# Two middle token chunks sorted by expert instead of by group, and late chunks taken between sorted pairs

## The chip, the cores and the metric

The kernel runs on one core of one Trainium2 chip. The metric is the device time of one execution in microseconds (us). Times of single instructions come from one profiled execution.

## What is computed

A vision tower of two layers on 64 images of 64 tokens (4096 tokens of width 256). Patch embedding, attention, a mixture of experts (8 experts in the program, one of them shared, top 2 of 7), a second attention, and a second mixture of experts, in which this change lies for the most part:

```python
# second layer: 16 experts in 4 groups; the best 2 groups, then the best 4 experts of those
scores = sigmoid(xf @ router_weight.T); s_choice = scores + router_bias
gidx   = top_k(sum of the top 2 of each group, 2)
topk   = top_k(s_choice masked to the two groups, 4)
w      = scores[topk] / (sum + 1e-20) * 2.5
out    = sum over e of combine[:, e] * (silu(x @ w_gate[e].T) * (x @ w_up[e].T)) @ w_down[e].T
h      = h + out
```

Products are made of three float32r products (high*high, low*high, high*low), so each tile is split into a high and a low part before it is used.

## The kernel before

Tokens lie in 32 blocks of 128. A mixture phase takes its blocks in chunks (`CHUNKS0` for the first layer, `CHUNKS` for the second). Work runs in pairs of two blocks. An "own" pair takes two blocks in token order: it is turned (transposed), gets its router logits, and in the first layer also the shared expert. When all own pairs of a chunk are through, DVE works out the routing of the chunk (`routing`, or `choose_experts` to `weigh_experts` in the first layer), and GpSimd scatters the chunk's rows to DRAM, sorted into lists, with one indirect DMA for each block and each list that a token is in. "Sorted" pairs are then loaded back from DRAM (`load`), multiplied with the weights of their list, and stored (`store`); GpSimd gathers the results, again with one indirect DMA for each block and choice, and DVE adds them to `h` (`combine`).

First layer (`routed_phase`): a list is an expert. Each sorted pair is one unit of work: 12 products for gate and up (`project`), 2 transposes of the hidden tile (`turn_hidden`), 6 products down (`down_product`). All 16 own pairs come first, then the 41 sorted pairs. The SP queue runs `load(x + 4)` and then `store(x - 3)`.

Second layer (`grouped_phase`, `Flow`): a list is a group of 4 experts. Each block sits in 2 lists (`GROUP_K`), its rows carry the 16 weights (`ROW` = 272 columns), and a sorted pair is 4 units, one for each member of the group, which add up in `p_y` and are stored once. Chunks of 8, 12, 8 and 4 blocks give 20, 28, 20 and 12 list blocks, thus 10, 14, 10 and 6 pairs, 160 units. `Flow.turn_at` sets the unit in which a pair is turned: for a pair behind a 4-unit pair the second unit of that pair; for a pair behind a one-unit item the unit of the item before that, so two units ahead of its own. In step `s` PE runs `project(s)`, then `turn_pair` of the pairs due, `find_groups` (two register loads that name the list of each block), `turn_hidden(s-1)`, `down_product(s-2)`. ACT runs `gate(s)`, `turned_high`, `hidden_high(s-1)`, `result(s-2)`. DVE runs `hidden_values(s)`, `turned_low`, `hidden_low(s-1)`, one piece of the pending `routing`, and a `combine` when due.

The SP queue of the second layer decides when a sorted pair's rows come in. Its loop (L1169 on) is

```python
for x in range(-LOADS, len(flow.of_move)):      # LOADS = 4
    if x + LOADS < len(flow.of_move):
        load(x + LOADS)
    if x >= 0:
        store(x)          # waits y_out >= x + 1, the result of pair x
        while sent < len(groups) and combine_at[sent] < flow.last_unit[flow.of_move[x]]:
            store_out(sent)
            sent += 1
```

Queues run in order: what stands behind a waiting `store` waits too. GpSimd's order is written out in `MOVES0` and `MOVES`; a `gather` keeps at most `RING` = 3 entries ahead of `combine`, an entry being two blocks, 4 indirect DMAs.

Of the kernel before, what the change touches and what calls it, by code (L numbers as in the profile page):

```python
# [18 lines left out]
F32 = mybir.dt.float32  # L19
# [47 lines left out]
GROUPS, GROUP_K = 4, 2  # L67
ROW = D + E1
# [359 lines left out]
class Pairs:  # L428
# [7 lines left out]
    def __init__(self, chunks, rooms, ahead, shared):  # L436
        own = lambda c: [("own", c, j) for j in range((chunks[c][1] - chunks[c][0]) // 2)]
        self.order = [pair for c in range(ahead) for pair in own(c)]
        for c in range(len(chunks)):
            late = own(c + ahead) if c + ahead < len(chunks) else []  # L440
            for j in range(rooms[c] // 2):
                self.order += [("sorted", c, j)] + late[j:j + 1]
        self.is_own = [kind == "own" for kind, _, _ in self.order]
        self.has_hidden = [shared or not own for own in self.is_own]
        self.owns = [sum(self.is_own[:i]) for i in range(len(self.order))]
        self.moves = [i - owns for i, owns in enumerate(self.owns)]
        self.hiddens = [sum(self.has_hidden[:i]) for i in range(len(self.order))]
        self.of_hidden = [i for i, has in enumerate(self.has_hidden) if has]
        self.of_move = [i for i, own in enumerate(self.is_own) if not own]
        self.first_move = self.of_move[0]  # L450
        self.moves_in = [sum(self.order[i][1] <= c for i in self.of_move) for c in range(len(chunks))]
        self.last_own = [max(i for i, pair in enumerate(self.order) if pair[:2] == ("own", c)) for c in range(len(chunks))]
# [7 lines left out]
def routed_phase(core, layer, experts, width, top_k, chunks, ahead, moves, combine_step, out=None, next_w=None):  # L460
# [8 lines left out]
    name = f"e{layer}_"  # L469
    shared = layer == 0  # L470
    real = experts - 1 if shared else experts
# [3 lines left out]
    plan = Pairs(chunks, rooms, ahead, shared)  # L475
    total = len(plan.order) + 3
    at_w = 0 if shared else E0
    groups = [(c, first) for c, (low, high) in enumerate(chunks) for first in range(low, high, 2)]
    LOADS, STORES = 4, 2
    with ExitStack() as ctx:  # L480
# [5 lines left out]
        wr, bias = core.wr[layer], core.bias[layer]  # L486
# [17 lines left out]
        nth = sb("nth", [P, top_k])  # L504
# [3 lines left out]
        if layer == 1:  # L508
            pick_ = [sb(f"pick{i}", [P, count, GROUPS]) for i in range(4)]
            wins = sb("wins", [P, BLOCKS, GROUPS])  # L510
# [18 lines left out]
        rounds, combined, stored = sem("rounds"), sem("combined"), sem("stored")  # L529
        if next_w is not None:  # L530
            next_here, next_split, stats = [sem("next_here0"), sem("next_here1")], sem("next_split"), sem("stats")
# [13 lines left out]
        def _(sp):  # L545
            for first in range(experts - 1, -1, -1) if shared else range(0, experts, 4):
                few = 1 if shared else 4
                for part in range(2):
                    sp.dma_start(w[part][:, first * WCOLS:(first + few) * WCOLS].bitcast(F32).rearrange("p (a n) -> p a n", n=WCOLS),
                                 d["we_parts"][part, at_w + first:at_w + first + few].rearrange("a p n -> p a n"))\  # L550
                        .then_inc(w_first if shared and first == real else w_here, 16)
# [21 lines left out]
            if out is not None:  # L573
                for g, (_, first) in enumerate(groups):
                    sp.wait_ge(combined, g + 1)
                    sp.dma_start(out[:, first:first + 2, :], core.h[:, first:first + 2, :]).then_inc(stored, 16)
                sp.wait_ge(stored, 16 * len(groups))

        @block.gpsimd
        def _(pool):  # L580
# [4 lines left out]
            if layer == 1:  # L585
                for g in range(GROUPS):
                    pool.memset(wins[:, :, g:g + 1], float(g))
# [6 lines left out]
            if layer == 0:  # L594
                core.clear_spent(pool)
# [37 lines left out]
        def _(act):  # L633
# [6 lines left out]
            def gate(i):  # L640
                h = plan.hiddens[i]
# [6 lines left out]
            def hidden_high(i):  # L648
                h = plan.hiddens[i]
                act.wait_ge(hid_turned, h + 1)  # L650
                if h >= 2:
                    act.wait_ge(down, h - 1)
                act.copy(hid[0][h % 2][:], p_ht[:, 0:2 * P]).then_inc(hid_hi, 1)

            def result(i):
                h, x = plan.hiddens[i], plan.moves[i]
# [5 lines left out]
            for s in range(total):  # L662
                for i in plan.steps(0, s):
                    turned_high(i)
                for i in plan.steps(1, s):
                    if plan.has_hidden[i]:
                        gate(i)
                for i in plan.steps(2, s):
                    if plan.has_hidden[i]:
                        hidden_high(i)  # L670
# [5 lines left out]
                for c in range(len(chunks)):  # L676
                    if s == plan.last_own[c] + 1:
                        if shared:
                            act.wait_ge(biased, c + 1)
                        else:  # L680
                            act.wait_ge(logits, plan.owns[plan.last_own[c]] + 1)
                        act.activation(scores_[:, 0:counts[c]], comb_[:, 0:counts[c]], ACT.Sigmoid).then_inc(sig, 1)
            if next_w is not None:
                norm.root(act, norm.EARLY)

        @block.vector
        def _(dve):
# [21 lines left out]
            def hidden_values(i):  # L709
                h = plan.hiddens[i]  # L710
# [4 lines left out]
            def hidden_low(i):  # L715
                h = plan.hiddens[i]
# [3 lines left out]
            def add_shared(i):  # L720
                n, h = own_block(i), plan.hiddens[i]
# [8 lines left out]
            def choose_groups(c):  # L730

                comb, scores, vals, *_ = rows_of(c)
                count = counts[c]
                pick = [part[:, 0:count] for part in pick_]
# [1897 lines left out]
```

## Time and profile before

| | us |
|---|---|
| median of 3 runs | 1984.54 |
| lowest, highest | 1981.78, 1986.18 |
| the profiled execution | 1974.37 |
| its span, first to last instruction | 1972.6 |
| PE busy in it | 1605.6 |
| first layer's mixture, about | 652 to 1030 |
| second layer's mixture | 1358 to 1973 |

PE is the TensorE matmul queue, PEld its weight loads, DVE VectorE, ACT ScalarE, POOL GpSimd, SP the sync engine, here a DMA queue. A timeline row is: start, length, engine, line, operation, output<-input, count, and in brackets the idle time before it with what ended it. An indirect DMA of GpSimd is a POOL row of about 1 us. PEclk is the granted TensorE clock, 1.00 being 2.4 GHz and 0.50 being 1.2 GHz.

### The profile page before, as it was taken

The page shows a single profiled execution, that of the slowest core. Times are in us where ns is not written, and L with a number is a line of the kernel's source. Part 1 is how long each engine was busy: PE and PEld are TensorE (multiplying, and loading weights), DVE is VectorE, ACT ScalarE, POOL GpSimd, SP SyncE. Part 2 cuts the span into 40 slices and gives each one's busy share as a digit, 9 for nine tenths or more (in the row PEclk, how much of TensorE's full clock was granted, in tenths as well). Part 3 has the DMA queues.
Part 4 walks back from the last instruction along what each step waited for, and adds up shares of the span by engine and source line. Part 5 has one row for each costly group of instructions (what it writes and reads, how often), then busy time and mean ns, then how long its engine had stood idle before and what let it go on. Part 6 is the DMA issues. An engine that isn't in the chain of part 4 may idle for free. (4 is left out here: it accounts for less than half of the span.)

```text
span 1972.6 us, 40622 instructions
## 1 busy us (share of the span) xinstructions
PE 1605.6 (81%) x15110; PEld 1419.5 (72%) x15110; DVE 1054.6 (53%) x2359; ACT 748.8 (38%) x1301; POOL 503.7 (26%) x437
## 2 busy tenths in 40 slices
PE   7979999999998764687627899887686887988974
PEld 6868888888887764676625676676576887977974
DVE  5636644655456533445446777775453364436442
ACT  5334344434444311253314766763122232332321
POOL 4054121112200044433442333331322203024031
PEclk9999999999999867797867989996597998989987
DMA  6236442133200321364420000004421222123222
GB/s 238 89 99 200 133 132 95 65 112 130 92 18 2 128 86 64 117 190 132 148 88 5 1 2 1 0 1 172 158 76 65 71 77 79 56 66 107 70 76 71
DMA packets 105922, 173.36 MB, mean 88 GB/s; under 512 B 11168, under 2 KB 78880, under 8 KB 104864
## 3 DMA queue, kind: packets, MB, share of 16 engines
q1 hardware_dynamic: 89296, 130.04, 19.6%
q0 software_dynamic: 14016, 40.39, 6.4%
q8 instruction: 121, 1.98, 0.4%
q10 hardware_dynamic: 2448, 0.61, 0.2%
q14 instruction: 41, 0.34, 0.1%
HBM read 87.51 MB, written 83.49 MB: 87 GB/s over the span
## 5 line engine op out<-in xcount | busy, mean ns | idle before, releaser
L115 PE MATMUL e_p_gu<-e_w_hi,e_xt_hi 128*128 (+1 forms) x868 | 267.2, 308 | 42.8 <-DVE e_xt_lo L701 30.4
L115 PE MATMUL e_p_gu<-e_w_hi,e_xt_lo 128*128 (+1 forms) x868 | 260.2, 300 | 7.3 <-issue 7.0
L115 PE MATMUL e_p_gu<-e_w_lo,e_xt_hi 128*128 (+1 forms) x868 | 260.2, 300 | 6.1 <-issue 5.8
L1318 DVE SCALAR_TENSOR_TENSOR e_gated<-e_gated,e_share,e_p_gu 128x128 f32<-128x128 f32 x320 | 96.9, 345 | 232.2 <-ACT e_gated L1242 207.0
L115 PEld LDWEIGHTS e_p_gu<-e_w_hi,e_xt_hi 128*128 128x128 f32 x868 | 181.5, 209 | 44.2 <-issue 42.4
L115 PEld LDWEIGHTS e_p_gu<-e_w_hi,e_xt_lo 128*128 128x128 f32 x868 | 181.1, 209 | 10.1 <-issue 10.0
L115 PEld LDWEIGHTS e_p_gu<-e_w_lo,e_xt_hi 128*128 128x128 f32 x868 | 181.8, 209 | 7.7 <-issue 7.7
L1242 ACT ACTIVATE e_gated<-e_p_gu 128x256 f32<-128x256 f32 x160 | 61.2, 384 | 287.7 <-PE e_p_gu L115 219.2
L115 PE MATMUL e_p_y<-e_w_hi,e_hid_hi 128*128 (+1 forms) x434 | 148.3, 342 | 6.3 <-issue 6.0
L1218 POOL DMA_INDIRECT e_xn<-results,e_row_of x64 | 64.8, 1012 | 314.8 <-issue 211.0
L115 PE MATMUL e_p_y<-e_w_lo,e_hid_hi 128*128 (+1 forms) x434 | 128.5, 296 | 2.0 <-issue 2.0
L115 PE MATMUL e_p_y<-e_w_hi,e_hid_lo 128*128 (+1 forms) x434 | 128.0, 295 | 1.7 <-issue 1.7
L1547 PE MATMUL e_p_ht<-ident,e_gated 128*128 128x128 f32 x320 | 65.1, 286 | 62.9 <-DVE e_hid_lo L1325 48.4
L115 PE MATMUL a_J<-a_xt_hi,w_qk_hi 128*128 128x512 f32 x256 | 106.9, 417 | 8.1 <-DVE a_xt_lo L1861 5.3
L115 PE MATMUL a_J<-a_xt_lo,w_qk_hi 128*128 128x512 f32 x256 | 101.2, 395 | 0.0
L115 PE MATMUL a_J<-a_xt_hi,w_qk_lo 128*128 128x512 f32 x256 | 101.2, 395 | 0.0
L2115 POOL TENSOR_TENSOR a_s<-a_s,a_total 128x1024 f32<-128x1024 f32 x32 | 60.9, 1902 | 152.1 <-DVE a_total L2283 151.4
L1843 DVE TENSOR_TENSOR a_ot_lo<-a_O,a_ot_hi 128x1024 fp32r<-128x1024 f32 x32 | 39.1, 1223 | 112.4 <-ACT a_ot_hi L1789 112.4
L115 PEld LDWEIGHTS e_p_y<-e_w_hi,e_hid_hi 128*128 128x128 f32 x434 | 88.2, 203 | 11.0 <-issue 8.0
L619 POOL DMA_INDIRECT e_xn<-results,e_row_of x64 | 64.9, 1015 | 113.0 <-DMA results<-e_y 74.9
L115 PEld LDWEIGHTS e_p_y<-e_w_lo,e_hid_hi 128*128 128x128 f32 x434 | 88.6, 204 | 2.1 <-issue 2.0
L1547 PEld LDWEIGHTS e_p_ht<-ident,e_gated 128*128 128x128 f32 x320 | 37.4, 145 | 73.1 <-issue 43.4
(332 smaller groups left out, 4422.6 us busy)
## 6 DMA issues: line engine op xcount, KB each, us to landing
results<-e_y SPq DMA_DIRECT2D x81, 256.0 KB
e_moved<-rows SPq DMA_DIRECT2D x40, 272.0 KB, 2.8
pa_x<-in_x SPq DMA_DIRECT2D x7, 1536.0 KB, 6.3
e_moved<-rows SPq DMA_DIRECT2D x41, 256.0 KB
w_qk_in<-in_we SPq DMA_DIRECT2D x24, 384.0 KB, 6.3
we_parts<-w_qk_in SPq DMA_DIRECT2D x24, 384.0 KB, 2.3
we_parts<-a_e_lo SPq DMA_DIRECT2D x24, 384.0 KB, 2.4
rows<-a_zero SPq DMA_DIRECT2D x8, 1088.0 KB, 5.9
```

What stands on the lines that cost most here:

```text
L115: mm = eng.matmul(out, lhs[a], rhs[b], start=start and n == 0, stop=stop and n == len(terms) - 1, skip_group_check=skip)
L619: pool.indirect_dma_start(out=yg[g % RING][:, n * top_k + k, :], out_offset=None, in_=d["results0"][c][0:rooms[c] * P], in_offset=bass.Ind ...
L1218: pool.indirect_dma_start(out=yg[g % RING][:, k, n, :], out_offset=None, in_=d["results"][c][0:rooms[c] * P], in_offset=bass.IndirectOffse ...
L1242: act.activation(gated[h % 2][:], p_gu[h % 2][:].rearrange("p (b n) -> p b n", n=2 * INNER)[:, :, 0:INNER], ACT.Silu)\
L1318: last = dve.scalar_tensor_tensor(gated[h % 2][:, b, :], gated[h % 2][:, b, :], share[x % 2][:, b, j:j + 1], up[:, b, :], ALU.mult, ALU.mult)
L1547: last = pe.transpose(p_ht[:, b * P:(b + 1) * P], gated[h % 2][:, b, :], core.ident[:])
L1843: dve.tensor_tensor(ot[1][:], p_o[:].rearrange("p i (j q) -> p j i q", q=SEQ), ot[0][:].bitcast(F32), ALU.subtract)\
L2115: pool.tensor_tensor(row_groups(s[c]), row_groups(s[c]), per_row(totals[c]), ALU.mult).then_inc(p_done, 1)
```

## The change

Second layer: `SORTED` says how each chunk is sorted. Chunks 0 and 3 stay by group. Chunks 1 (12 blocks) and 2 (8 blocks) go by expert: 16 lists of one member, 4 lists for each token, 256 columns for a row, 64 and 48 list blocks, so 32 and 24 pairs of one unit each. The weights of the choices are applied in `combine` (four `scalar_tensor_tensor` for a block), and an entry of `combine` and of the output's store is one block. Chunk 2's own pairs come after sorted pairs 4 and 5 of chunk 0, chunk 3's after sorted pair 4 of chunk 1. Chunk 1's routing takes 8 pieces at once. GpSimd scatters chunk 2 ahead of the gather of chunk 0. The SP loop quoted above, `LOADS` and `STORES` are as they were.

First layer: only two chunks of own pairs come first, and the third chunk's four own pairs come one by one after sorted pairs 8 to 11 of chunk 0. The routing becomes a generator: 10 pieces at once for chunks 0 and 1, the others one by one, and two at a step for chunk 2. The next attention's weights are split ahead of the first scatter. Combines are due later (`combine0`).

```diff
-MOVES0 = (("scatter", 0), ("scatter", 1), ("scatter", 2), ("weights", 0), ("gather", 0), ("gather", 1), ("gather", 2))
+MOVES0 = (("weights", 0), ("scatter", 0), ("scatter", 1), ("scatter", 2), ("gather", 0), ("gather", 1), ("gather", 2))
+OWN_FROM0 = 8
-MOVES = (("scatter", 0), ("scatter", 1), ("gather", 0), ("scatter", 2), ("gather", 1), ("scatter", 3), ("gather", 2), ("gather", 3))
+MOVES = (("scatter", 0), ("scatter", 1), ("scatter", 2), ("gather", 0), ("scatter", 3), ("gather", 1), ("gather", 2), ("gather", 3))
...
+BY_GROUP, BY_EXPERT = Sorting(GROUPS, E1 // GROUPS, GROUP_K, 2), Sorting(E1, 1, 4, 1)
+SORTED = (BY_GROUP, BY_EXPERT, BY_EXPERT, BY_GROUP)
...
-            late = own(c + 1) if 1 <= c < len(chunks) - 1 else []
+            late = own(c + 2) if c + 2 < len(chunks) else []
             for j in range(rooms[c] // 2):
-                self.order += [("sorted", c, j)] + late[2 * j:2 * j + 2]
+                self.order += [("sorted", c, j)]
+                if j >= 4:
+                    self.order += late[2 * (j - 4):2 * (j - 4) + 2]
...
-        self.turn_at = [-1 if i < 2 else self.first_unit[i - 1] + 1 if not self.is_own[i - 1] else self.last_unit[i - 2]
+        self.turn_at = [-1 if i < 2 else self.first_unit[i - 1] + 1 if self.last_unit[i - 1] > self.first_unit[i - 1] else self.last_unit[i - 2]
...
+        burst = [99, 8] + [0] * (len(chunks) - 2)
...
                 for n in range(*chunks[c]):
-                    for k in range(GROUP_K):
+                    for k in range(sorting[c].k):
                         pool.indirect_dma_start(out=d["rows"][c][0:rooms[c] * P],
...
+                if flow.order[i][1] in single:
+                    dve.tensor_tensor(gated[h % 2][:], gated[h % 2][:], up, ALU.mult).then_inc(valued, 1)
+                    return
...
+                    if by.members > 1:
+                        last = dve.tensor_tensor(rows, rows, got[:, 2 * k:2 * k + 2, :], ALU.add)
+                    else:
+                        last = dve.scalar_tensor_tensor(rows[:, 0, :], got[:, k, :], weight[:, first, k:k + 1], rows[:, 0, :], ALU.mult, ALU.add)
...
+def combine1(c, entry):
+
+    wait, apart = ((13, 1.9), (6, 1.9), (7, 2.2), (7, 2.2))[c]
+    return wait + math.ceil(apart * (entry + 1))
```

## Rows read from the trace of the kernel before

**Rows 1.** The page: span, then busy time of each engine

```profile
span 1972.6 us, 40622 instructions
PE 1605.6 (81%) x15110; PEld 1419.5 (72%) x15110; DVE 1054.6 (53%) x2359; ACT 748.8 (38%) x1301; POOL 503.7 (26%) x437
```

**Rows 2.** Busy time by stretch (PE, PEld, DVE, ACT, POOL, PEclk, DMA share, GB/s)

```profile
1450.00:1500.00 50.00, 26.16 (x191) 25.03 (x192) 17.00 (x62) 8.79 (x23) 23.62 (x24) 0.77 0.26 89
1500.00:1550.00 50.00, 49.06 (x393) 48.18 (x392) 22.67 (x70) 18.39 (x47) 0.00 (x0) 0.96 0.18 53
```

**Rows 3.** Timeline of ACT, second layer: the results of two grouped pairs in a row

```profile
1515.85 0.59 ACT L1257 COPY e_y<-e_p_y 128x512 f32<-128x512 f32 x1
1526.24 0.59 ACT L1257 COPY e_y<-e_p_y 128x512 f32<-128x512 f32 x1
```

**Rows 4.** Timeline of PE, second layer: a turned pair, then the last down products

```profile
1524.68 0.60 PE L1506 MATMUL e_p_xt<-ident,e_moved 128*128 128x128 f32 x4
...
1525.81 0.28 PE L115 MATMUL e_p_y<-e_w_lo,e_hid_hi 128*128 x1
1525.93 0.28 PE L115 MATMUL e_p_y<-e_w_hi,e_hid_lo 128*128 x1
```

**Rows 5.** Timeline of the SP queue behind the result at 1526.24

```profile
1526.86 0.36 SPq L1160 DMA_DIRECT2D results<-e_y  x1
1527.31 0.41 SPq L1154 DMA_DIRECT2D e_moved<-rows  x1
```

**Rows 6.** The load's line L1154, second layer, all 40: issue to landing

```profile
DMA to landing us min/median/max: 2.7/2.8/4.5
```

**Rows 7.** Timeline of ACT, first layer: first and last of 11 sorted pairs' gates

```profile
847.18 0.38 ACT L645 ACTIVATE e_gated<-e_p_gu 128x256 f32<-128x256 f32 x1 [0.79 <-PE e_p_gu L115]
...
878.87 0.38 ACT L645 ACTIVATE e_gated<-e_p_gu 128x256 f32<-128x256 f32 x1 [0.78 <-PE e_p_gu L115]
```

**Rows 8.** Timeline of POOL, second layer: first and last of a scatter's 24 DMAs

```profile
1463.99 0.98 POOL L1200 DMA_INDIRECT rows<-e_xn,e_row_of  x1 [53.27 <-DVE e_row_of L1421]
...
1493.64 0.98 POOL L1200 DMA_INDIRECT rows<-e_xn,e_row_of  x1 [0.30 <-issue]
```

**Rows 9.** Timeline of ACT, gates of the units around that scatter

```profile
1465.76 0.38 ACT L1242 ACTIVATE e_gated<-e_p_gu 128x256 f32<-128x256 f32 x1 [1.72 <-PE e_p_gu L115]
...
1480.29 0.38 ACT L1242 ACTIVATE e_gated<-e_p_gu 128x256 f32<-128x256 f32 x1 [11.42 <-remote]
...
1497.86 0.38 ACT L1242 ACTIVATE e_gated<-e_p_gu 128x256 f32<-128x256 f32 x1 [15.79 <-remote]
1498.39 0.40 ACT L1242 ACTIVATE e_gated<-e_p_gu 128x256 f32<-128x256 f32 x1
1503.90 0.38 ACT L1242 ACTIVATE e_gated<-e_p_gu 128x256 f32<-128x256 f32 x1 [3.46 <-PE e_p_gu L115]
```

**Rows 10.** Timeline of ACT, gates around a scatter of 16 DMAs from 1640.40

```profile
1642.22 0.38 ACT L1242 ACTIVATE e_gated<-e_p_gu 128x256 f32<-128x256 f32 x1 [1.72 <-PE e_p_gu L115]
...
1668.74 0.38 ACT L1242 ACTIVATE e_gated<-e_p_gu 128x256 f32<-128x256 f32 x1 [2.98 <-PE e_p_gu L115]
```

**Rows 11.** Timeline of POOL: first and last of 4 gathers of one entry

```profile
1913.27 0.99 POOL L1218 DMA_INDIRECT e_xn<-results,e_row_of  x1 [17.99 <-issue]
...
1917.18 1.00 POOL L1218 DMA_INDIRECT e_xn<-results,e_row_of  x1 [0.30 <-issue]
```

**Rows 12.** Timeline of ACT, gates around those 4 gathers

```profile
1911.27 0.38 ACT L1242 ACTIVATE e_gated<-e_p_gu 128x256 f32<-128x256 f32 x1 [0.86 <-PE e_p_gu L115]
...
1922.54 0.39 ACT L1242 ACTIVATE e_gated<-e_p_gu 128x256 f32<-128x256 f32 x1 [0.85 <-PE e_p_gu L115]
```

**Rows 13.** Timeline of DVE, first layer: first and last of chunk 2's routing

```profile
798.79 0.22 DVE L771 TENSOR_TENSOR e_comb<-e_comb,router_bias 128x64 f32<-128x64 f32 x1
...
808.69 0.29 DVE L845 TENSOR_REDUCE e_weight<-e_big 128x16 f32<-128x128 f32 x1
```

**Rows 14.** Timeline of PE, down products of a unit at the lower clock

```profile
1483.98 0.41 PE L115 MATMUL e_p_y<-e_w_lo,e_hid_hi 128*128 x1
1484.19 0.41 PE L115 MATMUL e_p_y<-e_w_hi,e_hid_lo 128*128 x1
```

More of the change, by code:

```diff
@@ new lines, in routing, with maxima @@
+            def routing(c):
+                comb, scores, vals, above, equal, rank, sel, restart = rows_of(c)
+                count, restart_e, placed = counts[c], restart_e_[counts[c]][:], equal
+                low, high = chunks[c]
+                wide, choices = [P, count, width], [P, count, top_k, width]
+                top, tally = top_[:, 0:count], tally_[:, 0:count]
+                inc, slot, p_rank, p_tot = (of_expert(part, c) for part in (inc_, slot_, p_rank_, p_tot_))
+                of_block = lambda a: a.rearrange("p (b e) -> p b e", e=1).broadcast_to(wide)
+                def maxima(of, start, end):
+                    for n in range(start, end):
+                        last = dve.max(top[:, n, :], of[:, n, :])
+                    then(last)
+                dve.wait_ge(logits, plan.owns[plan.last_own[c]] + 1)
+                dve.tensor_tensor(comb, comb, bias[1][:].rearrange("p (c n) -> p c n", c=1).broadcast_to(wide), ALU.add).then_inc(biased, 1)
+                yield
+                dve.wait_ge(sig, c + 1)
+                then(dve.tensor_copy(vals[:, :, 0:real], scores[:, :, 0:real]))
+                maxima(vals, 0, count // 2)
+                yield
+                maxima(vals, count // 2, count)
+                kth = top[:, :, top_k - 1:top_k].broadcast_to(wide)
@@ new lines, in sorted_phase @@
+        wins, kept_ = sb("wins", [P, BLOCKS, GROUPS]), sb("kept", [P, count, GROUPS])
+        sel_bf_ = sb("sel_bf", [P, lists], BF16)
+        top_, tally_ = sb("top", [P, count, 8]), sb("tally", [P, count])
+        ends_, both_ = sb("ends", [P, group_count, GROUP_K]), sb("both", [P, group_count])
+        nblk_, cum_, base_, ones = (sb(n, [P, experts]) for n in ("nblk", "cum", "base", "ones"))
+        starts = sb("starts", [P, count])
+        reached = sb("reached", [P, group_room, GROUPS + 1])
@@ L1183, in _ @@
             pool.memset(restart_[:], 1.0)
-            for part in restart_g_.values():
+            for part in restart_l_:
                 pool.memset(part[:], 1.0)
@@ L1191, in _ @@
             pool.memset(restart_[:, :, 0:1], 0.0)
-            for part in restart_g_.values():
+            for part in restart_l_:
                 last = pool.memset(part[:, :, 0:1], 0.0)
@@ new lines, in routing @@
+                dve.tensor_scalar(row_of[:, low:high, 0:by.k], ends, -1.0, None, ALU.add).then_inc(routed, 1)
+                yield
+                if by_group:
+                    far = reached[:, 0:rooms[c], 1:GROUPS + 1]
+                    upto = cum.rearrange("p (j e) -> p j e", j=1).broadcast_to([P, rooms[c], GROUPS])
+                    here = core.steps[:, 0:rooms[c]].rearrange("p (j e) -> p j e", e=1).broadcast_to([P, rooms[c], GROUPS])
+                else:
+                    far = work[0:1, 0:rooms[c] * lists].rearrange("p (j e) -> p j e", e=lists)
+                    upto = cum[0:1].rearrange("p (j e) -> p j e", j=1).broadcast_to([1, rooms[c], lists])
+                    here = core.steps[0:1, 0:rooms[c]].rearrange("p (j e) -> p j e", e=1).broadcast_to([1, rooms[c], lists])
@@ L1452, in _ @@
                 elif flow.unit(s):
+                    if pending is not None:
+                        for _ in pending:
+                            pass
                     take_logits(flow.units[s][0])
```

538 lines of the change are left out of this document (255 added, 283 removed).

## The prediction

> **What bounds the kernel now.** I read the page first. PE is busy for 81% of the span, no other engine for more than 53% [rows 1], so PE's work or PE's waits set the time. The two attentions are untouched; the change lies in the two mixture phases. There the busy times by stretch tell two kinds of time apart [rows 2]: between 1500 and 1550 PE is busy 49.06 of 50 us, between 1450 and 1500 only 26.16, and in that second stretch GpSimd is busy 23.62 us, with 24 operations. So while sorted pairs run undisturbed, PE is the bound, and while GpSimd issues indirect DMAs something else is. The timelines then price both.
>
> Undisturbed, a grouped pair of four units takes 1526.24 - 1515.85 = 10.39 us [rows 3]. A one-unit pair of the first layer takes (878.87 - 847.18) / 10 = 3.17 us [rows 7], which holds the turn of the pair and the register loads of its lists once for each unit.
>
> Disturbed, a scatter of 24 DMAs issues from 1463.99 to 1494.6, 1.29 us each [rows 8]. In that time ACT's gates come at 1465.76, 1480.29, 1497.86, 1498.39, 1503.90, with idle times of 11.42 and 15.79 us put to "remote" [rows 9]: PE, ACT and DVE all stand. Four units took 38.1 us instead of 10.39, a loss of 27.7. The scatter of 16 that begins at 1640.40 makes four units take 26.5 us, a loss of 16.1 [rows 10]. Four gathers alone, 1913.27 to 1918.2 [rows 11], make four units take 11.27, a loss of only 0.9 [rows 12]. So a long run of indirect DMAs costs 1.0 to 1.15 us each, about its whole length, and a run of four about 0.2 each. What does the holding the trace doesn't say; the times are enough for the sum.
>
> **Part 1, units.** Chunks 1 and 2 were 14 + 10 = 24 grouped pairs: 24 x 10.39 = 249.4 us go. They become 32 + 24 = 56 one-unit pairs. The work of each is that of the first layer's pair, and if PE could run it as there, 56 x 3.17 = 177.5 us would come, a gain of 72. I don't think that it can, because of a wait that the second layer's SP queue makes and the first layer's doesn't. In the quoted SP loop `load(k)` stands behind `store(k-5)`, and that store waits for the result of pair k-5. With four units a pair this is a dozen units ahead of use. With one unit a pair it isn't: pair k-5 has its down product in PE's step of pair k-3, and pair k is turned in the step of pair k-2, right behind `project`, which is twelve products or about 1.44 us at 0.12 each [rows 4]. Everything from the down product to the landed load must fit into these 1.44 us.
>
> It is a loop that I add up from rows. From the turn of a pair to the last down product of the same step 1.25 us (1524.68 to 1525.93) [rows 4]; from there to the start of the result's copy 0.31 and the copy 0.59 [rows 3, 4]; to the start of the store's issue 0.03 and to that of the load 0.45 [rows 5]; to its landing 2.8 [rows 6]; then the next turn. That is 5.43 us. The list's register loads now stand between turn and `turn_hidden`. An estimate from the first-layer pair's 3.17 less its 20 products and transposes and its turn at about 0.12 each (2.8) says up to 0.35 for them, partly beside the transposes, so I take 5.6. PE, which needs 3.17, DVE and ACT wait in this loop. Behind the waiting turn on PE are its own hidden transposes and down products, and so the next store: the loop holds itself. The first pair or so of each chunk finds its rows loaded; I take 53 pairs at 5.6 and 3 at 3.17: 306 us. Part 1: 306 - 249 = +57. The low bound is 53 x 5.2 for a loop without the register loads and with landings of 2.7 (-21), the high bound the lower clock, below.
>
> **Part 2, indirect DMAs.** The scatters of chunks 1 and 2 double, from 24 and 16 to 48 and 32; so do their gathers. The run of 48 comes in chunk 0's grouped pairs: 24 more at 1.29 = +31. The run of 32 (41.3 us) comes in the loop, where two steps of 5.6 fit in as two did in the 16 of rows 10: loss about 33 against 16.1, +17. Of the 40 added gathers the first twelve of a chunk stay one run; the others come four at a time, paced by the ring, and the nearest row is rows 12: between 0.2 and 1.15 each, 9 to 46 us, and I take 13, near the low end, since an entry's 5.2 us of issue is followed by a pause in combines due 1.9 units of 5.6 us apart. Sum +61. The bounds are 0, if the waits of the loop hide them all, and +94.
>
> The Trainium skill speaks against this term: the page "SBUF — State Buffer" says, in its consequences behind the table of ports, that DMA never contends with a compute engine. By that rule an added indirect DMA would cost PE nothing. The gates of the grouped units stand still beside the scatter [rows 8, 9], so the trace doesn't bear it out here.
>
> **Part 3, small ones.** Chunk 1's routing takes 8 pieces at once where it took one a step; DVE is late for its hidden values by some 8 us, of which PE's queue hides a few: +5. The output goes out in 16 one-block stores that fall into the loop's SP queue, at about 0.4 us of issue each as in rows 5: +6. The four multiplies a block in `combine` are DVE work; DVE needs under 4 us of a step of 5.6, so nothing. It would be late in a step of 3.17. The narrower rows (256 columns for 272) change the load by 6%; nothing. The tail behind the last unit stays: chunk 3 is as it was. Moving own pairs changes their place, not their work.
>
> **Part 4, the first layer.** The same 57 pairs and 128 indirect DMAs. The third chunk's routing, 10.2 us of DVE in one piece [rows 13], is spread over steps in which DVE has room: -6, at most -10. Splitting the weights moves 20 us of GpSimd work to where it had none; it ends before the first scatter. Later combines keep DVE from waiting for gathers behind which pairs queue: -6, between 0 and -20. What is late next is the runs of indirect DMAs, the same number as before. Sum -12, from -30 to +5.
>
> **The sum.** +57 +61 +5 +6 -12 = +117 us. Made against the profiled execution (1974.37) this gives 2091; that one lies 10.2 us under the median of 1984.54, and on the median it is about 2101. I say 2100.
>
> **Rivals.**
> (a) Not slower: the rows are there in time. If SP's load could be ahead as in the first layer, the 56 pairs run at 3.17 [rows 7]: 177.5 - 249.4 = -72, +61 +5 -12 (the stores of the output don't count) = -18, 1967. With DVE late, a few us more. It decides at the loop: once result, store issue, load and landing take less than 3.17 - 1.25 = 1.9 us it holds. For it: the first layer does so. Against: its loop has `store(x - 3)`, this one `store(x)`, and a landing alone is 2.7 at the least [rows 6]. Chance 0.09.
> (b) The added indirect DMAs cost nothing, since the loop waits anyway and the 48-run is shorter in effect: 2100 - 61 = 2039. For it: runs of four cost little [rows 12]. Against: the loop's steps pass through PE, ACT and SP, and in a long run all of them stand [rows 9]. It is what the skill's rule on the ports would give too. Chance 0.10.
> (c) PE's clock falls. It is 0.77 in the stretch with long stops and 0.96 in the one without [rows 2]. In the loop PE works 2.8 of 5.6 us. At 1.2 GHz products are 0.21 us apart instead of 0.12 [rows 14, 4]; the dozen between turn and last down product add 12 x 0.09 = 1.1 us a step, x 53 = +60: 2160. Chance 0.15.
> (d) The forecast, loop at 5.2 to 6, part of the gathers' cost: 0.66.
>
> **How the numbers follow.** The forecast with its own bounds goes from 2060 to 2140. To hold 8 in 10 the range takes in (b) at 2039 and (c) at 2160 and leaves (a) out: 2035 to 2165. A measurement of this kernel tells about 0.2%, 4 us. Slower by more than that: (b), (c), (d), together 0.91, less 0.02 for gains that I can't see, 0.89. Faster: most of (a), 0.08. Same: 0.03.
>
> **What would show it.** In the profile after: sorted pairs of chunks 1 and 2 with results 5.4 to 6 us apart, PE's turn (the transposes of `e_moved`) waiting for the load's DMA some 2 us in most of them, and PE's busy share near a half there. The load issued 0.45 us behind each store, as in rows 5. GpSimd runs of 48 and 32 with all engines standing. In the first layer no DVE stop of 10 us for the third chunk. The prediction is wrong if the turns don't wait for the load, or if the gates go on during a run of 48.

## The result and the profile after

The changed kernel takes 2127.06 us (median of 4 runs, 2122.57 to 2130.33) against 1985.36 for the kernel before (4 runs): ratio 1.0711, interval 1.0682 to 1.0741. The profiled execution spans 2124.7 us; that of before spanned 1972.6 [rows 1]. So the two profiles that are compared here lie 152.1 us apart, the medians 141.7.

The page of the changed kernel: its span, the busy time of each engine, and PE's busy tenths and granted clock in 40 slices.

```profile
span 2124.7 us, 39088 instructions
PE 1590.8 (75%) x14407; PEld 1386.7 (65%) x14438; DVE 1055.6 (50%) x2238; ACT 759.4 (36%) x1285; POOL 584.4 (28%) x519
...
PE   7989999999987649474588888672882766666774
...
PEclk9999999999998679687798989566895777777787
```

PE is busy for about as long as before (1590.8 against 1605.6 us) in a span 152 us longer. The added time isn't new work, it is waiting. (PE runs fewer products than before, 14407 records against 15110, but more of them at the lower clock: the granted clock of the whole run is 0.841, before it was 0.884.) A slice is 53 us. The last fourteen, from some 1380 us, are the second layer (7 2 8 8 2 7 6 6 6 6 6 7 7 4): two holes, the 2 from 1434 and the 2 from 1594, and between 1647 and 2019 a plateau of sixes and sevens, at a granted clock of 0.74 between 1646 and 2016. The holes are long runs of indirect DMAs, the plateau is the one-unit pairs.

Which wait it is, the load's line L1133 tells (duration of its issue, then the instructions that waited for its data, us and times):

```profile
L1133 SPq DMA_DIRECT2D e_moved<-rows x72: 359/415/1364, 1395.1 to 2041.0; - x72
...
  PE e_p_xt L1533: 116.8, 49
```

49 turns of a pair waited for their rows, 116.8 us in all. 47 of them belong to the 56 one-unit pairs between 1646 and 2016, 98.7 us, 2.1 each; the other two are first pairs of a chunk. The loop that the prediction described can be followed row by row over one pair. PE's timeline first: the turn (with its wait in brackets), the hidden transposes, the last down product and the next turn; then the result's copy on ACT, its store and the next load on the SP queue, and the next result.

```profile
1667.19 0.66 PE L1533 MATMUL e_p_xt<-ident,e_moved 128*128 128x128 f32 x4 [2.63 <-DMA e_moved<-rows]
1668.50 0.41 PE L1574 MATMUL e_p_ht<-ident,e_gated 128*128 128x128 f32 x2 [0.65 <-issue]
...
1669.76 0.41 PE L136 MATMUL e_p_y<-e_w_hi,e_hid_lo 128*128 x1
...
1674.09 0.66 PE L1533 MATMUL e_p_xt<-ident,e_moved 128*128 128x128 f32 x4 [1.44 <-DMA e_moved<-rows]
```

```profile
1670.21 0.59 ACT L1237 COPY e_y<-e_p_y 128x512 f32<-128x512 f32 x1 [0.90 <-PE e_p_y L136]
...
1677.42 0.59 ACT L1237 COPY e_y<-e_p_y 128x512 f32<-128x512 f32 x1 [1.07 <-PE e_p_y L136]
```

```profile
1670.83 0.36 SPq L1139 DMA_DIRECT2D results<-e_y  x1
1671.29 0.41 SPq L1133 DMA_DIRECT2D e_moved<-rows  x1
```

The result at 1670.21, its store at 1670.83, the load behind it at 1671.29; the turn that waits for that load comes at 1674.09, and the next result is at 1677.42: 7.21 us a pair. Over the rows between 1655 and 1850 the medians of the pieces are: turn to hidden transposes 1.28, from there to the last down product 1.53 (0.92 to 0.96 where products are 0.12 us apart, which is the full clock), to the copy 0.45 (0.32), to the store 0.61, to the load 0.46, to the next turn 2.9.

The other change is the long run of indirect DMAs. The timeline of GpSimd, first and last of chunk 1's scatter, now 48 DMAs, and the gates of ACT beside it (those of before are [rows 8, 9]):

```profile
1429.97 0.98 POOL L1180 DMA_INDIRECT rows<-e_xn,e_row_of  x1 [36.41 <-DVE e_row_of L1421]
...
1491.31 0.98 POOL L1180 DMA_INDIRECT rows<-e_xn,e_row_of  x1 [0.30 <-issue]
```

```profile
1444.59 0.38 ACT L1222 ACTIVATE e_gated<-e_p_gu 128x256 f32<-128x256 f32 x1 [6.65 <-remote]
1476.44 0.38 ACT L1222 ACTIVATE e_gated<-e_p_gu 128x256 f32<-128x256 f32 x1 [31.21 <-remote]
1498.25 0.38 ACT L1222 ACTIVATE e_gated<-e_p_gu 128x256 f32<-128x256 f32 x1 [16.52 <-remote]
```

One grouped pair takes 64.4 us there (results at 1437.35 and 1501.73), where the two behind it take 10.0. PE doesn't only wait for ACT's gates there. Inside one `project`, where the code waits for no other engine between the products, they come 2.8 us apart there (undisturbed 0.12 or 0.21):

```profile
1489.03 0.37 PE L136 MATMUL e_p_gu<-e_w_lo,e_xt_hi 128*128 x1 [2.41 <-issue]
1491.83 0.37 PE L136 MATMUL e_p_gu<-e_w_hi,e_xt_lo 128*128 x1 [2.43 <-issue]
```

The second layer in stretches, from the first issue of chunk 0's scatter to the last result of each chunk:

| | before | after | difference |
|---|---|---|---|
| chunk 0 (10 grouped pairs) | 167.5 | 221.3 | +53.8 |
| chunk 1 (14 grouped, 32 one-unit pairs) | 185.7 | 255.6 | +69.9 |
| chunk 2 (10 grouped, 24 one-unit pairs) | 133.0 | 165.1 | +32.1 |
| chunk 3 (6 grouped pairs) | 73.0 | 86.5 | +13.5 |
| behind it | 23.3 | 23.3 | 0 |

That is +169.3. The second layer's first scatter starts at 1372.88 instead of 1390.02, and already the first layer's last result comes at 984.0 instead of 1001.4: -17.1 from the first layer. Together +152, the difference of the spans.

Not all of a row is stops and loop. The four own pairs of chunk 2 now stand in chunk 0. They make two of its intervals between results 14.57 and 16.72 us where undisturbed ones are about 10.4, so some 10.5 us of chunk 0's +53.8 are work that chunk 1 had before.

### The profile page after: what moved, and what is told of

Read it like the earlier page. It is cut to its first block and busy times, and to the rows that moved or that the text cites. A ratio compares the mean times of both kernels' runs of the same rounds, so it can differ in the third digit from the quotient of the medians.

```text
span 2124.7 us, 39088 instructions
## 1 busy us (share of the span) xinstructions
PE 1590.8 (75%) x14407; PEld 1386.7 (65%) x14438; DVE 1055.6 (50%) x2238; ACT 759.4 (36%) x1285; POOL 584.4 (28%) x519
## 5 line engine op out<-in xcount | busy, mean ns | idle before, releaser
L136 PE MATMUL e_p_gu<-e_w_hi,e_xt_hi 128*128 (+1 forms) x708 | 234.7, 332 | 42.6 <-DVE e_xt_lo L699 29.7
L136 PE MATMUL e_p_gu<-e_w_lo,e_xt_hi 128*128 (+1 forms) x708 | 226.9, 321 | 17.5 <-issue 17.3
L136 PE MATMUL e_p_gu<-e_w_hi,e_xt_lo 128*128 (+1 forms) x708 | 225.8, 319 | 13.4 <-issue 13.4
L1198 POOL DMA_INDIRECT e_xn<-results,e_row_of x104 | 105.2, 1012 | 332.1 <-DVE h L1463 132.2
L1180 POOL DMA_INDIRECT rows<-e_xn,e_row_of x96 | 96.0, 1000 | 198.7 <-DVE e_row_of L1421 170.3
L1533 PE MATMUL e_p_xt<-ident,e_moved 128*128 128x128 f32 x288 | 56.3, 328 | 117.0 <-DMA e_moved<-rows 116.8
L1272 DVE TENSOR_TENSOR e_xt_lo<-e_p_xt,e_xt_hi 128x512 fp32r<-128x512 f32 x88 | 60.8, 691 | 155.1 <-ACT e_xt_hi L1215 134.7
L1533 PEld LDWEIGHTS e_p_xt<-ident,e_moved 128*128 128x128 f32 x288 | 37.3, 163 | 128.8 <-DMA e_moved<-rows 128.4
L1215 ACT CAST e_xt_hi<-e_p_xt 128x512 fp32r<-128x512 f32 x88 | 51.5, 586 | 193.3 <-PE e_p_xt L1533 159.2
L1574 PEld LDWEIGHTS e_p_ht<-ident,e_gated 128*128 128x128 f32 x240 | 29.6, 162 | 116.8 <-issue 104.9
L2143 POOL TENSOR_TENSOR a_s<-a_s,a_total 128x1024 f32<-128x1024 f32 x32 | 60.9, 1904 | 152.8 <-DVE a_total L2311 152.1
L1296 DVE TENSOR_TENSOR e_gated<-e_gated,e_p_gu 128x256 f32<-128x256 f32 x56 | 23.6, 421 | 158.3 <-ACT e_gated L1222 146.6
```

The lines of the kernel that those rows point to most:

```text
L136: mm = eng.matmul(out, lhs[a], rhs[b], start=start and n == 0, stop=stop and n == len(terms) - 1, skip_group_check=skip)
L1180: pool.indirect_dma_start(out=d["rows"][c][0:rooms[c] * P], out_offset=bass.IndirectOffsetOnAxis(ap=row_of[:, n, k:k + 1], axis=0), in_=ow ...
L1198: pool.indirect_dma_start(out=yg[g % RING][:, k * sorting[c].entry + n, :], out_offset=None, in_=d["results"][c][0:rooms[c] * P], in_offse ...
L1215: act.copy(xt[0][i % 2][:], p_xt[i % 2][:]).then_inc(xt_hi, 1)
L1272: dve.tensor_tensor(xt[1][i % 2][:], p_xt[i % 2][:], xt[0][i % 2][:].bitcast(F32), ALU.subtract).then_inc(xt_lo, 1)
L1296: dve.tensor_tensor(gated[h % 2][:], gated[h % 2][:], up, ALU.mult).then_inc(valued, 1)
```

## Experiments

The four runs of a group shared one chip and the runs of the kernel before there. The kernel before took 1984.6 us on the first chip (A), 1806.6 on the second (B) and 1974.0 on the third (C). Chip A agrees with the 1985.4 beside the result, so the runs there are set against the changed kernel's 2127.06; whether it is the same chip isn't known. That the chips would differ so much I had not expected; it became the best evidence of the study.

### First group, chip A

**e1_load_ahead.** The SP loop as in the first layer:

```diff
-            for x in range(-LOADS, len(flow.of_move)):
+            for x in range(-LOADS, len(flow.of_move) + 3):
                 if x + LOADS < len(flow.of_move):
                     load(x + LOADS)
-                if x >= 0:
-                    store(x)
-                    while sent < len(entries) and combine_at[sent] < flow.last_unit[flow.of_move[x]]:
+                if x >= 3:
+                    store(x - 3)
+                    while sent < len(entries) and combine_at[sent] < flow.last_unit[flow.of_move[x - 3]]:
                         store_out(sent)
```

> The changed kernel with one edit: the second layer's SP loop issues load(x + 4) ahead of store(x - 3) instead of ahead of store(x), as the first layer's loop does, so that a load stands behind the store of the pair eight before it and no longer five. My theory: the 56 one-unit pairs are held by the loop result, store, load, landing, turn. Then the turn's wait for e_moved (116.8 us over 49 pairs) nearly goes, the pairs' intervals fall from 7.2-7.4 us to 3.2-3.8, and the time falls by 150 to 200 us, to some 1925 to 1975. Rival 1, the added indirect DMAs are the main cost: the time falls by less than 60 us. Rival 2, the lower clock and the register loads hold the pairs by themselves: intervals stay over 5 us and the time falls by 60 to 120.

Measured: 1974.59, ratio to before 0.995 (0.9925 to 0.9976). That is 152 us less than the changed kernel, inside the range, and about the time of before. Who waits for the load now, and three results in a row on ACT:

```profile
  PE e_p_xt L1533: 1.1, 1
```

```profile
1673.53 0.59 ACT L1237 COPY e_y<-e_p_y 128x512 f32<-128x512 f32 x1 [0.34 <-PE e_p_y L136]
1676.77 0.59 ACT L1237 COPY e_y<-e_p_y 128x512 f32<-128x512 f32 x1 [0.42 <-PE e_p_y L136]
1679.93 0.59 ACT L1237 COPY e_y<-e_p_y 128x512 f32<-128x512 f32 x1 [0.42 <-PE e_p_y L136]
```

The wait falls from 116.8 us to 1.1, the median pair from 7.2 to 3.16. In a stretch of this kernel where GpSimd is all but idle (busy us of PE, PEld, DVE, ACT, POOL; granted clock; DMA share; GB/s) and in the changed kernel's loop:

```profile
1673.00:1690.00 17.00, 16.54 (x134) 15.28 (x133) 11.22 (x34) 10.09 (x22) 0.73 (x1) 1.00 0.53 157
```

```profile
1655.00:1850.00 195.00, 128.37 (x683) 113.34 (x682) 56.97 (x153) 56.26 (x116) 11.96 (x12) 0.75 0.28 87
```

PE is busy for 97% at the full 2.4 GHz against 66% at 0.75 of it. So the lower clock was a consequence of the loop, not a cause beside it: the same products at the same place in the code run at the full clock once the rows are there. Both rivals fall. The stretch of 17 us is a quiet one, though. Over all of chunks 1 and 2 (1600.88 to 1867.80) the clock is 0.83, PE is busy for 72%, and the 56 pairs take 266.9 us, 4.8 each: the stops beside indirect DMAs are still there (one pair takes 45.8 us).

**e2_groups.**

```diff
-SORTED = (BY_GROUP, BY_EXPERT, BY_EXPERT, BY_GROUP)
+SORTED = (BY_GROUP, BY_GROUP, BY_GROUP, BY_GROUP)
```

> The changed kernel with all four chunks of the second layer sorted by group again; kept are the first layer's new order, the routing in pieces, the order of scatters and gathers and the SP loop. Theory: the whole loss belongs to the sort by expert, and what is kept is worth -17 us (the first layer ends that much earlier in the trace) and about +5 for the burst of routing: 1965 to 1980. Rival: the new order of the own pairs, the routing in pieces or the stores of the output in the SP queue cost tens of us by themselves: over 2000.

Measured: 1978.55, 0.9966 (0.9941 to 0.9992), 6 us under before. The second layer begins at 1372.5 as in the changed kernel (-17.6), and takes 17.0 us more than before, of which 5.8 lie ahead of the first result. The whole loss belongs to the sort by expert. The rival, over 2000, falls. Of the other 11 us I have only an argument: chunk 2's scatter of 16 and chunk 0's first 12 gathers now issue as one run, 1552.8 to 1588.9, where before they were two.

**e3_lists_first.**

```diff
+                if flow.hidden(s + 1) and flow.units[s + 1][1] == 0:
+                    find_lists(flow.units[s + 1][0])
                 for i in flow.turns(s):
                     turn_pair(i)
-                if flow.hidden(s + 1) and flow.units[s + 1][1] == 0:
-                    find_lists(flow.units[s + 1][0])
```

> The changed kernel with the lists of a pair looked up on PE ahead of the turn of the next pair instead of behind it, so that the register loads fall into the wait for the load and no longer between the turn and the hidden transposes. Theory: the loop that holds the pairs gets shorter by the 0.65 us that PE idles in front of the hidden transposes, 53 times: -25 to -37 us. If the loop doesn't hold the pairs: no change, within 5 us.

Measured: 2113.42, 13.6 us less than the changed kernel. Right in sign, about half of what I expected. In the profile chunks 1 and 2 take 400.7 us instead of 420.7, so 20 less, while the second layer starts 5 us later than in the changed kernel's. The turn of a pair and the hidden transposes behind it:

```profile
1673.96 0.66 PE L1533 MATMUL e_p_xt<-ident,e_moved 128*128 128x128 f32 x4 [2.66 <-DMA e_moved<-rows]
1674.46 0.38 PE L1574 MATMUL e_p_ht<-ident,e_gated 128*128 128x128 f32 x2
```

0.50 us apart instead of 1.31; the median over the loop went from 1.28 to 0.91, the period from 7.2 to 6.8. There are two values: 0.50 where the products behind are at the full clock, 0.91 where they are at the lower one, and in the changed kernel it was 1.28 at either. So the register loads were 0.4 us of the loop in most pairs, 0.8 in some, and time taken out of the loop shortens it: it is the bound. Pairs at the full clock are now 5.5 to 5.7 us apart.

**e4_paced.**

```diff
-                for n in range(*chunks[c]):
+                for at, n in enumerate(range(*chunks[c])):
+                    if c in PACED and at > 0:
+                        pool.wait_ge(projected, PACED[c][0] + int(PACED[c][1] * at))
...
+PACED = {1: (17, 2.0), 2: (49, 1.5)}
```

> The changed kernel with the scatters of chunks 1 and 2 in groups of four indirect DMAs: before each group but the first GpSimd waits until PE has projected two units more (chunk 1) or one and a half (chunk 2). The same 80 DMAs, no long run. Theory, a run costs what the run is long but four cost almost nothing: the 64.4 us pair in chunk 0 goes (about -45 us), the stop beside the run of 32 goes (about -20): 2055 to 2085. Rival, each indirect DMA costs PE the same 1.0 to 1.15 us however they are spaced: within 10 us of the changed kernel.

Measured: 2089.75, 37.3 us less than the changed kernel, 5 short of the range. Chunk 0 takes 187.2 us instead of 221.3 (-34), chunk 1 7.8 less. Where the groups were held apart it worked, though not for nothing: the first intervals of chunk 0 are 13.3, 17.8, 13.1, 11.3 and 23.6 us, where without any stop they are 10.8, 10.9, 10.6, 10.0 and 14.6 (e9_no_scatter1 on chip B, below). That is 22 us for 48 DMAs, 0.46 each, against 1.2 in one run. Chunk 2's waits were mostly met already when its routing came, and 24 of its 32 DMAs still issued in one run, 1547.4 to 1578.8. The rival, a fixed price for each DMA, is out on this chip.

### Second group, chip B

**e5_narrow** and **e9_no_scatter1.** In the first the run of 48 sends 16 of 256 columns, in the second it is left out.

```diff
-    in_=own_rows(n)[:, 0:sorting[c].width()], in_offset=None, ...
+    in_=own_rows(n)[:, 0:16 if c == 1 else sorting[c].width()], in_offset=None, ...
```

> The changed kernel, with chunk 1's scatter (the run of 48 indirect DMAs) sending 16 columns of each row instead of 256: as many DMAs and rows, one sixteenth of the bytes; the rest of chunk 1's rows stays zero, which is the part of the computation that it leaves out. Theory A, the issue on GpSimd or the number of rows holds the engines: the pair that took 64.4 us in chunk 0 still takes 50 to 65. Theory B, the moved bytes hold them: it takes under 25.

```diff
                 if move == "scatter":
-                    scatter(c)
+                    if c != 1:
+                        scatter(c)
...
-                if j == 0:
+                if j == 0 and c == 1:
+                    sp.wait_ge(routed, c + 1)
+                elif j == 0:
                     sp.wait_ge(scattered[c], 16 * counts[c] * sorting[c].k)
```

> The changed kernel with chunk 1's scatter left out (its 48 indirect DMAs; chunk 1's rows stay zero, so its part of the result is left out). It prices the whole run: the nearest number is the one pair of 64.4 us where ten others take 10 to 11 without a routing beside them. Theory: 50 to 58 us less than the changed kernel, 1.0 to 1.2 us for each DMA. Rival, PE makes up part of the stop later, for instance in the wait for chunk 2's scatter: under 35 us less.

Measured: 1932.56 and 1932.46, one run each. Both leave out a part of the computation. Neither expectation can be judged as it was meant, since on this chip there is no stop to take away: the pair beside the run takes 10.9 us with the narrow DMAs and 10.9 without any. The stretch of the 48 DMAs in e5_narrow, and the same stretch without them in e9_no_scatter1 (columns as above; the fifth is GpSimd):

```profile
1360.00:1422.00 62.00, 57.62 (x475) 55.58 (x474) 37.05 (x113) 24.76 (x57) 47.62 (x48) 1.00 0.17 47
```

```profile
1360.00:1422.00 62.00, 57.78 (x477) 55.76 (x476) 36.96 (x113) 24.72 (x57) 0.00 (x0) 1.00 0.15 45
```

PE does 57.62 us of work beside 47.62 us of indirect DMAs, and 57.78 without any. On the chip of the result it was 18.16 us of work in 65 (stretch 1430 to 1495 of the changed kernel, granted clock 0.63). It isn't the small width either: in e6_both, below, the run of 48 is full width, and while its first 40 issue PE stays busy:

```profile
1353.00:1404.00 51.00, 47.28 (x383) 46.19 (x383) 29.72 (x79) 17.26 (x44) 39.13 (x40) 0.97 0.39 131
```

GpSimd's own issue takes the same 1.31 us a step on both chips (1359.61 to 1420.96 here, 1429.97 to 1491.31 there, for 47 steps). Nor are the bytes moved more slowly where the engines stand. In 50 us of the full-width run GpSimd's DMA queue moved 4.98 MB at 27.1% of the DMA engines' time in the changed kernel (1435 to 1485), and 4.99 MB at 27.3% in e6_both (1354 to 1404).

What follows for the loop is clean: with no stops, chunks 1 and 2 take 221.3 + 163.7 = 385.0 us in e9_no_scatter1, with a median of 7.28 and 7.21 a pair, as on the other chip, and a mean of 6.9, since the first pairs of each chunk find their rows loaded.

**e8_groups_paced.** All chunks by group, as in e2_groups, and the scatters of chunks 1 and 2 in fours.

> All four chunks of the second layer sorted by group, as in the run before with that edit, and the scatters of chunks 1 and 2 (24 and 16 indirect DMAs) in groups of four with a wait for PE's units between them. Theory, runs cost their length and fours little: the two stops of some 24 and 16 us shrink to some 8 together: 1978.6 less 20 to 32 = 1946 to 1958. Rival, a DMA costs the same however it is spaced: 1970 to 1985.

Measured: 1801.06 beside 1806.62, 0.9968 (0.9942 to 0.9993). e2_groups was 0.9966 on chip A, so the pacing did nothing here, where there is nothing for it to do. It was hardly tried either: 12 of chunk 1's 24 DMAs and all 16 of chunk 2's still issued in one run. The expected numbers were for chip A. What the run gives is the price of the grouped pairs without stops: chunks 1 and 2 take 152.4 + 107.0 = 259.4 us, the median pair 10.45 and 10.47. Chunk 0 shows the four own pairs of chunk 2 once more, 14.57 and 16.72 us.

**e6_both.** Loads ahead, lists ahead, paced scatters, chunk 0's combines later:

```diff
+PACED = {1: (17, 1.7), 2: (52, 3.0)}
...
-    wait, apart = ((13, 1.9), (6, 1.9), (7, 2.2), (7, 2.2))[c]
+    wait, apart = ((22, 1.9), (6, 1.9), (7, 2.2), (7, 2.2))[c]
```

> The changed kernel with everything that the first four runs spoke for: loads ahead of store(x - 3), lists looked up ahead of the turn, scatters of chunks 1 and 2 in groups of four (1.7 and 3 units apart), and chunk 0's combines due nine units later so that its gathers have time. Theory, the gains add: 1974.6 less 37 (pacing, as measured in the slower loop), less up to 13 (lists) = 1925 to 1940, faster than both kernels. Rival, in the quick loop of 3.2 us a pair there is no room for the groups beside PE's work and each group of four costs what it did in the run: 1955 to 1980.

Measured: 1742.60, ratio 0.9674 (0.9634 to 0.9714), on a chip where the numbers expected for chip A don't apply. Chunk 1's scatter wasn't paced in fact, all 48 DMAs issued in one run. The 56 pairs take 107.6 + 74.7 = 182.3 us, 3.26 each. It also shows what my edit costs. ACT and the SP queue in chunk 0:

```profile
1420.04 0.58 ACT L1240 COPY e_y<-e_p_y 128x512 f32<-128x512 f32 x1 [15.22 <-DMA results<-e_y]
```

```profile
1388.70 0.47 SPq L1140 DMA_DIRECT2D results<-e_y  x1
1416.46 0.36 SPq L1134 DMA_DIRECT2D e_moved<-rows  x1
1416.87 0.46 SPq L1140 DMA_DIRECT2D results<-e_y  x1
```

The first load of chunk 1 now stands ahead of three stores of chunk 0 and waits for the whole scatter of 48 (its last DMA issues at 1414); no result can be copied until a store has gone. ACT waits 15.22 us, and PE does only 5.4 us of work from 1405 to 1420. A queue entry that is moved forward brings its wait along.

### Third group, chip C

**e10_changed**, the changed kernel unedited.

> The changed kernel itself, unedited, beside the kernel before on one chip. The first four runs and the next four were on two chips; on the first the kernel before takes 1985 us and long runs of indirect DMAs stop PE, ACT and DVE, on the second it takes 1807 and nothing stops beside them. Theory: the loop that holds the one-unit pairs is the same everywhere, the stops belong to the chip. On a chip with stops 2115 to 2130 (ratio 1.065 to 1.073); on a chip without, 1925 to 1937, a ratio of 1.066 to 1.072, with 7.2 to 7.4 us a one-unit pair and the pairs of chunk 0 at 10 to 11 beside the run of 48.

Measured: 2133.48 against 1974.04, 1.0824 (1.0771 to 1.0878). The time is 3 us over the range expected for a chip with stops, the ratio over its range because this chip runs the kernel before 11 us quicker. It has the stops: chunk 0 takes 220.2 us, the pair in the loop 7.24 and 7.39. So two of the three chips behave as the one of the result. The changed kernel's own ratio on chip B wasn't run; the nearest are the two kernels of 1932.5, 1.070 of before there.

**e11_ahead**, e1_load_ahead again.

> The changed kernel with load(x + 4) issued ahead of store(x - 3), a second time. On a chip with stops as before, 0.995 of the kernel before. On a chip without stops the 56 pairs take 3.17 each: 56 x (7.3 - 3.17) = 231 us less than the changed kernel, some 1700, that is 0.94 of the kernel before. If the stores and the output's stores in the SP queue or DVE hold the pairs in their turn, 4 to 5 us a pair: 1750 to 1800.

Measured: 1965.96, 0.9963 (0.9937 to 0.9988), as on chip A.

**e12_ahead_lists** is e11_ahead with the lists ahead of the turn, as in e3_lists_first.

> As the run before, and the lists looked up ahead of the turn. PE is the bound in the quick loop, where both places of the register loads stand in its queue: within 8 us of the run before, on any chip. If the register loads hide in the wait for the transposes' copy only when they stand behind the turn: 20 to 35 us slower.

Measured: 1954.58, 0.9931 (0.9896 to 0.9966). That is 11 us less than e11_ahead, where I expected at most 8. The intervals of the two ratios overlap. But eight of its ten times lie below all ten of e11_ahead (1951.26 to 1959.06 against 1960.56 and more) and two above (1973.84, 1977.8), so a small gain is likely and not certain.

**e13_both**, the kernel of e6_both.

> Loads ahead, lists ahead, scatters of chunks 1 and 2 in groups of four. On the chip without stops it took 0.967 of the kernel before. On a chip with stops, theory: pacing takes back about 37 us of the run before, 1930 to 1945 against 1985 (0.97 to 0.98); rival: the pacing does nothing in the quick loop, within 10 us of the run before. On a chip without stops: pacing has nothing to take back; 1735 to 1750, and the run before is the quicker one, since groups three units apart make chunk 0's gathers late.

Measured: 1907.98, 0.9665 (0.9621 to 0.9709). Better than expected: 46.6 us under e12_ahead_lists. The two profiled executions are only 29.8 us apart; there chunk 0 takes 39 less (196.8 instead of 236.1), chunk 1 7.6 less, chunk 2 13.3 more. Here chunk 1's scatter did split, into runs of 4 to 12. But the kernel differs from e12_ahead_lists in two edits, the pacing and the later combines of chunk 0, and no run tells them apart. It takes 3.3% less than the kernel before on a chip with stops and on one without; the changed kernel's 2133.48 on this chip it beats by 10.6%.

## Why the prediction was right, and where it wasn't

Direction and size were right: 2100 forecast, 2127 measured, inside 2035 to 2165. The mechanism of the largest term was right too, its size wasn't, and that the total came so close is partly luck: one term was 69 us too small, another 23 too large. Between the profiles the sum was +117 and +152 came; the medians are 142 apart. The terms, each with what the runs gave:

| term | forecast | measured | from |
|---|---|---|---|
| one-unit pairs for grouped ones | +57 | +126 | 385.0 - 259.4, chip B, no stops |
| added indirect DMAs | +61 | +38 | what is left of 169.3 less 125.6 and 5.7 |
| routing in a burst | +5 | +5.7 | first result 51.1 instead of 45.5 us behind the first scatter |
| output stores in the SP queue | +6 | about +7, inside the first line | mean store to load 0.58 us, median 0.46, times 56 |
| first layer | -12 | -17 | start of the second layer |

**The mechanism of part 1 held.** `load` behind `store(x)`, the turn waiting for the DMA, the loop that holds itself: 47 of 56 turns wait, and undoing that one order takes 152 us back (e1_load_ahead against the changed kernel's 2127.06), and 167.5 on chip C, where both ran side by side. Of its pieces the tail was forecast well: copy to store 0.61 (0.62 forecast), store to load 0.46 (0.45), load to turn 2.9 (2.8).

**The step that was mis-sized** is the front of the loop, from the turn to the result's copy. I took 1.25 + 0.31 from a grouped pair in the middle of busy work [rows 3, 4], plus 0.17 for the register loads. At the full clock it is 1.28 + 0.92 + 0.32 = 2.5 us. In the grouped pair the hidden transposes start 0.43 us behind the turn, in the loop 1.28 behind it, with an idle time of 0.65 in front of them. e3_lists_first shows how much of that the register loads are, 0.8 us at the full clock and 0.4 at the lower; with them out of the way pairs at the full clock are 5.5 to 5.7 us apart, near the 5.43 that I had added up without them. I had named that piece, and sized it from a kernel where PE's queue has work ahead; there it hides. In the loop nothing is ahead.

**Rival (c) was no rival but a part of the forecast.** In most steps of the loop the clock is 1.2 GHz: the same pieces take 1.28 + 1.53 + 0.45. A pair at the full clock takes 6.4, at the lower one 7.2, so 0.8 us; I had said 1.1 us a step and given it a chance of 0.15 as a case of its own. When the bound becomes a wait the clock can go too, as it did here, and the sum should have held both. The 56 pairs take 385 us and not 306, about 7.1 for each of the 53; the grouped pairs with their own pairs between were 259 and not 249; together +126 instead of +57.

**Part 2 was too high by 23, and its places were wrong.** It offset a third of part 1's error. Chunk 0 pays 53.8 - 5.7 - 10.5 for the own pairs = +38, for 31 forecast: the doubled run costs 54 us for some 27 (one pair of 64.4 us where those behind it take 10.0, for the 27.7 of the gates in [rows 9]), 1.1 a DMA as forecast, and some 9 are the last pair of the chunk, 19.8 us, beside which the run of 32 now begins. I had put that run into the loop. (My 33 us for it was also a slip: 41.3 less two steps of 5.6 is 30.) In chunks 1 and 2 the stops fell: 420.7 - 385.0 = 36 us after, and 318.7 - 259.4 = 59 before, of which 10.5 are the own pairs, so 49. With the loop there they fell although the DMAs doubled, as if a loop that waits anyway hides a part of them; rival (b) was right for that half and wrong for chunk 0. Chunk 3 pays 13.5, which I had not forecast; it has more gathers beside it (40 between 2020 and 2124), and on chip B it takes 61.7 us against 60.1 with all chunks by group, which speaks for the stops here too.

**Part 2 as a property of hardware was wrong.** I took the stops of [rows 8 to 10] for what a run of indirect DMAs does to the engines. On chip B it does nothing of the kind. The Trainium skill's page "SBUF — State Buffer", section "Who interferes with whom", says that DMA never contends with a compute engine; chip B agrees (57.62 us of PE work with the run, 57.78 without). On the chips of the result, A and C the engines do stand beside such a run (one pair takes 64.4 us, on C 65.5), though no run shows that it is the moved data that they contend with. The prediction was blind to the difference between chips, and right about the chip that it was measured on.

**Rival (a)** put the time at 1967 if SP's load were ahead. e1_load_ahead and e11_ahead, built that way, give 1975 and 1966. Its point of decision was right, the forecast that it isn't reached too. That DVE would be late in a step of 3.17 didn't happen where nothing stops the pairs: the median pair of chunk 1 is 3.16, and on chip B all 56 average 3.26 (e6_both).

**Of the signs that I had named** these came: the turns wait 2.1 us for the load on average, the load is issued 0.46 behind each store, all engines stand in the run of 48, and in the first layer the third chunk's routing is spread over 833 to 860 us. Two didn't: results are 7.2 us apart and not 5.4 to 6, and PE is busy for 66% in the loop and not near a half, both by the front of the loop and the clock.

**What stays open.** Which resource holds the engines beside a long run on chips A and C. In the rows a gate of ACT comes 24 us behind a `project` that had ended by 1452.1, but PE has its own late products too, 2.8 us apart inside a `project`, so it isn't ACT alone. Slower moving of the bytes isn't it (27.1% and 27.3% of the DMA engines' time on the two kinds of chip). Whether bytes, rows or the issue does it was what e5_narrow was to tell, and it met the chip that has no stops. Why that one lacks them isn't known either: one chip, seen in one group of runs, and what else differs with it wasn't looked at.

## What to carry to other kernels

When a unit of work is made shorter, add up every loop that runs through a queue and compare it with the new period of the work; a load that stands behind a store of a recent result is such a loop, and moving it ahead in that queue was worth as much as the whole change had cost. In such a loop take no duration from a stretch where the engines had work queued, and reckon with the lower clock: here it was 0.8 us of 7.2. A load moved ahead takes its wait along, so see what then stands behind it.

## What the runs showed of the hardware that I had not expected

Chips can differ in a whole mechanism, not by a per cent: the same program takes 1985.4 us beside the result, 1984.6 on chip A, 1974.0 on C and 1806.6 on B. The two kernels without the wide run of 48 span 1930.0 us there where the changed kernel spans 2124.7: 70 us less by the second layer's start, 125 less in it. A number forecast from a trace holds, for such a kernel, for a chip of the kind that the trace was taken on. And PE's granted clock followed the waits closely: 0.75 in the loop at 66% busy, 1.00 in the same code at 97%. The stops don't show in GpSimd (1.31 us a step on both kinds of chip) or in what its queue moves; they show only in the engines beside it.
